# Offsets of a deformable convolution by 32-row matmul tiles from one copy of its input

## The reference, cut to what matters

```python
x = x + L0_conv(gn(x))            # 3x3 depthwise and two channel mixes, folded into one 3x3 conv ("conv1")
x = x + L1_conv(gn(x))            # deformable 3x3 conv
# L1_conv:
off    = conv3x3(v, w_off)        # 64 channels: a row and a column offset for each channel and pixel
rows   = clip(off[..., 0] + row, 0, 127);  cols = clip(off[..., 1] + col, 0, 127)
mapped = bilinear(v, rows, cols)  # each channel samples itself at its own offsets
out    = conv3x3(mapped, w_conv) + b_conv       # "conv2"
# gn(v): each channel of each image less its mean, over its standard deviation
```

## Time and profile before

| | |
|---|---|
| device time, median of 3 runs (lowest to highest) | 728.01 us (725.72 to 731.11) |
| span of the profiled execution, first to last instruction | 724.3 us |
| PE busy | 684.9 us (95%) |
| DVE, POOL, ACT busy | 525.0, 478.0, 465.9 us |
| DMA traffic | 115.6 MB |

### The profile page before, as it was taken

The page is one execution under the profiler, slowest core; times in us unless marked ns, Lnnn a source line. Parts: engine busy times, 40 slices in busy tenths (PEclk is TensorE's granted clock), DMA queues, the critical chain, the costliest instruction groups (busy, mean ns, idle before and its releaser), DMA issues.

```text
span 724.3 us, 10746 instructions
## 1 busy us (share of the span) xinstructions
PE 684.9 (95%) x3500; PEld 244.5 (34%) x3500; DVE 525.0 (72%) x1037; ACT 465.9 (64%) x809; POOL 478.0 (66%) x413
## 2 busy tenths in 40 slices
PE   4799979999999699999999999999999999999986
PEld 4333333333333233333333333333333333333322
DVE  3587988779935858657985598657984775578892
ACT  7487777676728824766567666577656775577860
POOL 4004867888594844868758666886658668787760
PEclk9999999999999989999999999999999999999999
DMA  8958927889459895699948997599957626477555
GB/s 140 186 109 149 136 60 164 174 178 205 121 129 247 163 199 131 157 223 173 201 108 194 200 219 163 132 231 179 207 132 173 158 60 143 116 163 179 123 126 135
DMA packets 140189, 115.64 MB, mean 160 GB/s; under 512 B 15168, under 2 KB 114016, under 8 KB 140128
## 3 DMA queue, kind: packets, MB, share of 16 engines
q1 hardware_dynamic: 116096, 103.12, 68.2%
q10 hardware_dynamic: 24032, 11.78, 9.0%
HBM read 31.59 MB, written 16.78 MB: 67 GB/s over the span
## 4 chain that ended last, share of the span: by engine, by line
PE 61%; SPq 11%; DVE 4%; ACT 3%; POOL 3%; issue 2%; DMA 2%; DVEq 0%; POOLq 0%; ACTq 0%
PE off_ps L781 30%; PE c_ps L670 26%; SPq L388 3%; SPq L469 3%; PE c_ps L681 2%; PE c_ps L685 2%; SPq L451 2%; DMA mapb<-mapa 1%; SPq L420 1%; DVE other_row L1422 1%; ACT other_row L975 1%; ACT off_abs L988 1%; POOL row_diff L1199 1%; SPq L461 1%; PE c_ps L689 1%
## 5 line engine op out<-in xcount | busy, mean ns | idle before, releaser
L1422 DVE COPY_PREDICATED other_row<-down_ps,row_diff 128x768 f32<-128x768 int32 x128 | 124.7, 1027 | 114.8 <-ACT down_ps L986 114.8
L781 PE MATMUL off_ps<-x1a,wo 128*64 128x512 f32 x768 | 176.8, 594 | 0.8 <-DVE other_row L1434 0.8
L781 PE MATMUL off_ps<-x1b,wo 128*64 128x512 f32 x768 | 176.1, 592 | 0.0
L670 PE MATMUL c_ps<-xb,w 128*64 128x512 f32 x336 | 149.8, 593 | 4.2 <-DVE xb L1495 2.0
L670 PE MATMUL c_ps<-mapb,w 128*64 128x512 f32 x336 | 150.8, 594 | 1.6 <-DVE x1a L1407 1.6
L672 PE MATMUL c_ps<-xa,w 128*64 128x512 f32 x336 | 149.8, 593 | 0.0
L975 ACT ACTIVATE other_row<-row_diff 128x768 f32<-128x768 f32 x128 | 100.8, 835 | 67.4 <-POOL row_diff L1201 46.5
L1216 POOL TENSOR_TENSOR other_row<-other_row,x_strips 128x512 f32<-128x512 f32 x48 | 57.2, 1192 | 128.1 <-DVE other_row L1434 128.1
L672 PE MATMUL c_ps<-mapa,w 128*64 128x512 f32 x294 | 131.7, 594 | 0.0
L986 ACT ACTIVATE down_ps<-off_ps,bias_o 128x512 f32<-128x512 f32 x64 | 41.9, 655 | 108.0 <-PE off_ps L781 100.5
L1217 POOL TENSOR_TENSOR other_col<-other_col,other_row 128x512 f32<-128x512 f32 x64 | 86.3, 1349 | 31.4 <-DVE other_row L1434 31.3
(11 more groups left out here) (135 smaller groups left out, 990.3 us busy)
## 6 DMA issues: line engine op xcount, KB each, us to landing
mapa<-mapped SPq DMA_DIRECT2D x224, 65.0 KB, 2.0
x1b<-x1a SPq DMA_DIRECT2D x28, 520.0 KB, 6.5
mapb<-mapa SPq DMA_DIRECT2D x28, 520.0 KB, 8.3
out_dram<-x1a SPq DMA_DIRECT2D x49, 256.0 KB, 4.7
xb<-in_x_dram SPq DMA_DIRECT2D x48, 256.0 KB, 9.0
xa<-in_x_dram ACTq DMA_DIRECT2D x40, 256.0 KB, 7.3
x_strips<-x1a SPq DMA_DIRECT2D x112, 81.2 KB, 2.1
x_strips<-x1a SPq DMA_DIRECT2D x112, 65.0 KB, 2.1
```

The source lines that it names most:

```text
L670: nc.tensor.matmul(bank[0:64, :], weights[:, kx, :], rows_b[:, of, kx:kx + W], start=(kx == 0), stop=(kx == 2))
L781: last = nc.tensor.matmul(off_ps[k % 2][64 * t:64 * t + 64, CH * n:CH * n + CH], wo[wpar][:, kx, side:side + 2 * C], rows[:, b:b + 7:2, kx ...
L1422: last = dve.copy_predicated(other_row[n][:, :, KR // 2 * odd:KR // 2 * odd + KR // 2, :], bass.AP(tensor=rows.tensor, offset=rows.offset ...
```

## The change

Offsets are computed from `x1a` alone. A matmul takes one row class, 32 partitions, and one tap (ky, kx) with weights of 32 rows x 64 columns; there are nine taps and no zero rows. Four row classes and two output halves make eight such tiles. Two chunks, now the left and the right half of the same rows, are worked as one **set** of 72 matmuls: for each ky, three kx, and within these the four row classes, each of which writes another bank of the set's four. A row class goes on with the next ky only when the class that wrote its next bank before has finished (`row_step`, waits of PE for PE). `x1b`, its DMAs and ACT's writes of it are gone.

The tables now name sets (4 an image): four groups stand behind each set. `off_ps` has three pairs of banks and `c_ps` one bank. A set uses two pairs; behind it, jobs take `c`, then the two banks x and y of the third pair, which held the second chunk of the set before, and `c` again (`BANKS`). So a set starts when its first bank pair's jobs (x, y) have been moved out and the first chunk of the set before is used.

ACT and DVE work a set's two chunks one after the other. ACT does both chunks' parts, then the set's conv1 groups, then `sum_far`; `pad_x1` stands behind set 2's two chunks. DVE adds two conv2 groups between the chunks, one inside the second chunk and one behind it; `x1_norm` stands ahead of set 2, `x_stats` behind set 2 and `x_norm` behind set 3 (for image 0: behind sets 0 and 1). POOL has four buffers of row differences instead of two. At the end some rows are copied a chunk earlier, since left and right halves now end together.

```diff
-    NEXT_CONV1 = [[0, 1], [2, 3], [4, 5], [6, 7], [], [], [], []]
-    LAST_CONV2 = [[], [], [], [], [0, 1], [2, 3], [4, 5], [6, 7]]
+    NEXT_CONV1 = [[0, 1, 2, 3], [4, 5, 6, 7], [], []]
+    LAST_CONV2 = [[], [], [0, 1, 2, 3], [4, 5, 6, 7]]
+    END_CONV2 = [[], [0, 1, 2], [3, 4, 5], [6, 7]]
+    BANKS = ["", "c", "xc", "xyc", "cxyc", "ycxyc"]
...
+    def bank_number(name, u):
+        return 6 if name == "c" else 2 * ((2 * u + 2) % 3) + (name == "y")
...
-        x1b = sb("x1b", [P, BL, WP])
-        wo = [sb(f"wo{n}", [P, 3, P]) for n in range(2)]
+        wo = [sb(f"wo{n}", [P, TAPS, 2 * C]) for n in range(2)]
-        off_ps = [pb(f"off_ps{n}", [P, 2 * CH]) for n in range(2)]
+        off_ps = [pb(f"off_ps{n}", [P, 2 * CH]) for n in range(3)]
         down_ps = pb("down_ps", [P, CH])
-        c_ps = [pb(f"c_ps{n}", [P, 4 * W]) for n in range(3)]
+        c_ps = pb("c_ps", [P, 4 * W])
...
             for i in range(NB):
                 if prev:
-                    sp.wait_ge(off_done, NK * i)
-                    copy_x1b(i % 3, 1)
...
                 if nxt:
                     sp.wait_ge(x1_pads, i + 2)
-                    sp.wait_ge(off_done, NK * i + 4)
-                    copy_x1b((i + 1) % 3, 0)
                     sp.wait_ge(mapped_ready, NK * i + 4)
                     for half in range(2 if prev else 1):
                         move_strips(sp, i + 1, half)
...
-            def offsets(wpar, par, k):
-                side = 2 * C * (k // 2 % 2)
-                for n, rows in enumerate((x1a[par], x1b)):
-                    for kx in range(3):
-                        for t in range(2):
-                            b = 2 * NJ * t + NJ * (k // 4) + k % 2
-                            last = nc.tensor.matmul(off_ps[k % 2][64 * t:64 * t + 64, CH * n:CH * n + CH],
-                                                    wo[wpar][:, kx, side:side + 2 * C],
-                                                    rows[:, b:b + 7:2, kx:kx + W],
-                                                    start=(kx == 0), stop=(kx == 2))
+            def offsets(i, wpar, par, s, tiles):
+                half, parity = s // 2, s % 2
+                for ky in range(3):
+                    order = [(3 + ky + n) % 4 for n in range(4)]
                     for kx in range(3):
+                        for r in order:
+                            c = (r - ky) % 4
+                            side, n, shift = c % 2, c // 2, (c + ky) // 4
+                            if ky > 0 and kx == 0:
+                                pe.wait_ge(row_step[(r - 1) % 4], 4 * (NS * i + s) + 2 * ky)
+                            for t in range(2):
+                                b = 2 * NJ * t + NJ * half + parity + shift
+                                last = nc.tensor.matmul(tiles[side][64 * t:64 * t + 64, CH * n:CH * n + CH],
+                                                        wo[wpar][Q * r:Q * r + Q, 3 * ky + kx, :],
+                                                        x1a[par][Q * r:Q * r + Q, b:b + 7:2, kx:kx + W],
+                                                        start=(ky == 0 and kx == 0), stop=(ky == 2 and kx == 2))
...
+                    if s == 2:
+                        if nxt:
+                            pad_x1(i + 1, (i + 1) % 3)
```

More of the change, by code:

```diff
@@ L122, in deformable_preact_kernel, with place_in @@
-    place = {job: n for n, job in enumerate(job_order)}
+        jobs += [("x1", i + 1, m) for m in conv1_groups(i, s)]
+        jobs += [("x1", i + 2, m) for m in further_groups(i, s)]
+        jobs += [("c2", i - 1, m) for m in conv2_places(i, s)]
+        return jobs
+    bank_of, held_before, in_bank = {}, {}, {}
+    def place_in(job, banks):
+        bank_of[job] = banks
+        held_before[job] = [in_bank[b] for b in banks if b in in_bank]
+        for b in banks:
+            in_bank[b] = job
@@ L124, in deformable_preact_kernel @@
+    last_jobs = [("c2", NB - 1, m) for m in range(8)]
+    for n, job in enumerate(last_jobs):
+        place_in(job, [bank_number("xyc"[n % 3], NS * NB - 1)])
     ctx = ExitStack()
@@ L604, in _ @@
                     wait_apart(conv1_done, 8 * v)
-                    wait_apart(off_done, NK * v)
+                    for side in range(2):
+                        wait_apart(off_done[side], 4 * NS * v)
                     for half in range(2):
@@ L643, in _ @@
             pe.wait_ge(s_setup["dve"], 2)
[L644 removed]
+            nc.tensor.matmul(general_banks[0][0:32, 0:32], soft_e[:, 1, :], ident[0:32, 0:32], start=True, stop=True)\
               .then_inc(s_setup["pe"], 1)
@@ L759, in job_of @@
                 kind, i, m = job
-                ps = bank(job)
+                for earlier in held_before[job]:
+                    wait_freed(earlier)
+                ps = bank(*job)
                 if kind == "b1":
@@ L1017, in clamp, with copy_end @@
                 act.activation(to, of, ACT.Copy).then_inc(clamped, 1)
-            def bank(*job):
-                return c_ps[place[job] % 3]
-            def copy_left(which_rows, chunks):
+            def copy_end(which_rows, cols, chunks):
                 act.wait_ge(end_pads, 1)
@@ L1025, in copy_left @@
                 act.wait_ge(mapped_ready, NK * (NB - 1) + chunks)
-                for q, t, o, shifted in which_rows:
-                    to, rows = end_row(q, t, o, shifted, slice(0, 1 + WQ))
-                    last = act.activation(to, rows, ACT.Copy)
-                return last
-            def copy_right(which_rows, chunks):
-                act.wait_ge(mapped_ready, NK * (NB - 1) + chunks)
                 for which in which_rows:
-                    to, rows = end_row(*which)
+                    to, rows = end_row(*which, cols)
                     last = act.activation(to, rows, ACT.Copy)
@@ new lines, in _ @@
+                    if s == END_BIAS + 1 and not nxt:
+                        conv2_bias(i, i % 2, bank("b2", i, 0))
+                    offset_parts(i, b)
+                    for n, m in enumerate(groups):
+                        if n == 3:
+                            sum_far(i, a)
+                        x1_group(i + 1, (i + 1) % 2, (i + 1) % 3, m, i + 1 >= 3, bank("x1", i + 1, m))
+                    for m in further_groups(i, s):
+                        x1_group(i + 2, i % 2, (i + 2) % 3, m, False, bank("x1", i + 2, m))
@@ L1203, in row_steps @@
                                    ALU.subtract).then_inc(diff_ready, 1)
-            row_steps(0, 0)
+            for pair in range(2):
+                row_steps(0, pair)
             for i in range(NB):
@@ L1484, in _, with copy_end_rows @@
-                    if after and k == (5 if i else 2):
-                        x_stats(i + 2, 1)
-                    if after and k == (5 if i else 3):
+                    if after and s == (2 if i else 0):
+                        for half in range(2):
+                            x_stats(i + 2, half)
+                    if after and s == (3 if i else 1):
                         x_norm(i + 2, i % 2)
-            def copy_end_rows(which_rows, chunks):
+            def copy_end_rows(which_rows, cols, chunks):
```

430 lines of the change are left out of this document (198 added, 232 removed).

## The result

The changed kernel takes 733.69 us (median of 20 runs, 728.81 to 738.48), the kernel before, in runs beside it, 725.62 us (20 runs, 721.57 to 733.84): a ratio of 1.0115 (95% interval 1.0092 to 1.0138), 1.2% slower, where 1.4% faster was forecast. The profiled execution took 738.19 us, 4.5 above its median; its span is 736.3 us, 12.0 more than the span before, while the medians are 8.1 apart. So what is read from this one trace makes the change look some 4 us dearer than it is. The times of the twenty runs go with their granted clock, from 728.81 us at 0.969 to 738.48 at 0.957.

The account below looks back on a forecast made before the run. TensorE was taken to bound the kernel, with the store loop binding after the change. Start +6, four periods -8.8 and end -7 gave -9.8 on the 724.3 us span: 714.5, median 718 us; own range 707 to 731.

Parts of the forecast that it names:

- The set, 8.7 us: Offsets on TensorE: a set takes 8.7 us where two chunks took 10.32, 1.6 us less.
- row tiles share a path: Rival, offset matmuls: row tiles overlap only partly, a round 0.56 instead of 0.43, 763 us, or about 915; chance 0.08.
- the sets gain nothing: Rival, offset sets: steps cost 1.3 each, a set takes 10.3 us, period 85.3, 747 us; chance 0.07.
- The store loop binds: Per image, pads, strips, store, conv1, next pads: this loop overtakes TensorE by 2 to 4 us, summing to 80.4 us.
- TensorE binds, 699 us: Rival, middle images: the store loop does not bind, TensorE does, period 78.1 us, 699 us in all; chance 0.17.
- The period of 82.1 us against 84.3: Time between successive images' first conv1 writes into `x1a` (W): 82.1 us instead of 84.3, giving -8.8 over four images.
- A wait near 4 us costs 1.7 more: TensorE's fourth conv1 group: after waiting near 4 us, the lowered clock adds 1.7 us to each image's period.
- Pads to W, "38.6": From pads' end through SP's strips and store to conv1's first write into `x1a` (W): 38.6 us, 43.1 before.
- The SP rival: SP's queue stays long, strips over 23.5 us, the store wait grows: period 86.1, 741 us; chance 0.18.
- Start, "+6": Images before image 3: its first conv1 write (W) comes 6 us later, at 224 us instead of 218.
- End, "-7": From image 7's first conv1 write (W) to POOL's last chunk: 136.5 us instead of 143.5.
- The 3.7 us that made 718 of the span: Whole kernel: the median stands 3.7 us above the span, turning a forecast span of 714.5 into 718 us.

Follow-up runs that it names:

- run 2: Changed kernel with ACT's pads of the next image placed between set 2's two chunks instead of behind both: 708.93 us, ratio 0.9759 to the kernel before.
- run 7: Changed kernel with the third conv1 group behind set 0 computed twice, for images from 3 on: 728.29 us, ratio 1.0030 to the kernel before.
- run 4: Kernel before, with the first half of an image's store issued by SP ahead of the first sixteen mapa moves: 724.53 us, ratio 0.9978.
- run 5: Changed kernel with pads between set 2's chunks and, in images 0 and 1, lent PSUM banks emptied between a set's chunks: 706.77 us, ratio 0.9733 to before.
- run 8: Changed kernel with early pads, lent banks emptied early, and four conv1 groups computed twice during images 0 and 1: 705.34 us, ratio 0.9701 to before.
- run 1: Changed kernel with the first half of an image's store issued by SP ahead of the first sixteen mapa moves: 722.62 us, ratio 0.9967 to before.

## Why the prediction was wrong

The mechanism was the forecast one, and the sign was wrong, because the forecast was a small difference of large terms, and every term that missed came out on the same side. By its own steps, on the spans (forecast -9.8, measured +12.0), the 21.8 us between them are 10.8 in the period, 5.1 in the start, 4.4 in the end and 1.5 in the tail. These are figures of one execution, 4.5 us above its median; from which term those 4.5 come is open.

- **The set, 8.7 us: right.** 8.77 measured, rounds 0.43 apart with eight row and column tiles, which refutes "row tiles share a path" and "the sets gain nothing". The 0.08 for a restart behind a step stood on no row, but the step came out as taken: 0.25 more than a round (446.50 to 447.18).
- **The Trainium skill's 3.07** ("TensorE: Matmul & The Clock Gate", Part 3, "Measured speedup vs the span model") would have made a round 0.56, as the prediction estimated from it; this trace has 0.43, so the measurement decides against it here.
- **The store loop binds: right, shown by runs 2 and 7**; TensorE was the bound before (run 4). "TensorE binds, 699 us" falls for this kernel. With the pads at their early place the period is near that rival's (79.4 for 78.1), the time 708.9.
- **The period of 82.1 us against 84.3: this is the step that failed.** It is 84.8, so four images cost +2.0 us instead of giving 8.8. Two terms were too small. "A wait near 4 us costs 1.7 more", taken from the earlier trace rows, is 2.6 by run 7's period. On TensorE itself the group takes 5.3 us instead of 2.6, since in three of the five images the whole group was slow, not part of it, and set 1 behind it takes 9.1 (405.28 to 414.37). Pads to W, "38.6", is 40.2: the strips take 22.0 us where 21.3 was meant and the `mapa` moves 10.8 where the earlier trace rows had 10.06, 1.5 of the 1.6. W to the pads is 44.9 where 41.8 and 1.7 were reckoned, nearly all of it the clock. (This image takes 85.1 us, 44.9 and 40.2; the mean of four is 84.8.) The margin that the forecast built on was 2.2 us an image, no wider than these errors.
- **The SP rival (741 us, slower)** came nearest in time, but its condition failed: the strips take 22.0 us, not over 23.5. What the loop takes over the forecast is 1.4 us from W to the pads and 1.6 in SP's list, of which the strips are 0.7. The pads' place was priced rightly; run 2 shows what it is worth.
- **Start, "+6": it is +11.1** (229.13 for 218.03). The estimate had image 1 4 us late and did not price the stops of sets that wait for a lent pair, 12.4 us in five, or the clock behind them: the granted clock is 0.83 from 100 to 120 us, 0.91 before. Run 2 takes 3.6 us of it off by the pads' place alone, run 5 another 2.8 by freeing lent pairs, run 8 2.2 with the clock kept: 8.6 of the 11.1. The rest was not taken apart.
- **End, "-7": it is -2.6** (W of image 7 to POOL's last chunk is 140.9 us, 143.5 before; the parts named for the 136.5 add up to 136.2), and the tail 27.1 instead of 25.6. Of this the trace shows the cold group (again) and image 7's second set, which waits 5.70 us for DVE and then takes 11.39 us instead of 8.8:

```profile
646.26 11.39 PE L816 MATMUL off_ps<-x1a,wo 32*64 32x512 f32 x144 [5.70 <-DVE other_row L1440]
```

The end was not tried by a run of its own.

The 3.7 us that made 718 of the span came of three runs; over twenty the median of the kernel before is 725.62, 1.3 above its span. The range (696 to 750) held the time. A sounder reading of the same rows would have asked which step in the loop the change makes later: the pads stood behind one chunk's parts before and stand behind two, 10.1 us after the offsets, and the forecast priced this (10.3) without asking what it would be worth to undo.

## What to carry to other kernels

When a change frees the engine that binds, add up the loop just beneath it, through every queue, before counting the gain; if the margin is 2 us in 84, forecast no change, and look for the step of that loop that the change itself makes late. Here three small fills behind the second of two batched chunks held a gain of 25 us. Batching two units of work into one made the hand-over of PSUM pairs coarser here, and most of the longer stops of the matmul engine that came of it also cost slow matmuls behind them.

## What the hardware showed

- Matmul tiles of 32 rows x 64 columns, four in rows and two in columns, ran fully beside one another: 144 instructions of 512 columns in 8.8 us. Within a set eight start together, the next eight 0.43 us later (406.51, 406.95 and 407.38 in image 4's set 1), the spacing that two tiles side by side had before. The round behind a wait for TensorE's own earlier matmuls started 0.68 us after the one ahead of it (446.50 to 447.18), twice a set.
- The length of a stop alone did not decide the clock behind it. Stops of 0.74 and 1.62 us left the matmuls behind them at their full pace, and so did one of 2.84 us in the changed kernel (its set at 127.75 takes 8.81 us) and one of 3.46 us in run 7 (TensorE by time):

```profile
229.81 0.64 PE L698 MATMUL c_ps<-xb,w 128*64 128x512 f32 x1 [3.46 <-ACT x1a L967]
...
230.29 0.59 PE L698 MATMUL c_ps<-xb,w 128*64 128x512 f32 x1
```

A stop of 2.12 us in the changed kernel did not (its set at 88.06 takes 10.53 us, with a granted clock of 0.50 from 89 to 91 us), nor did those of 3.29 (run 5), 3.49 (run 1), 3.78 and 5.70 us (changed kernel), with starts up to 0.85 us apart. Matmuls whose results are thrown away kept the level (runs 7 and 8).
- Two copies of 520 KB within SBUF landed 4.6 to 8.1 us after their issue in four images of the changed kernel, with eight loads of 256 KB issued behind them on the same queue. With four more loads issued beside them on ACT's queue one took 11.2 us in run 1.
